# Half of the modulation weights on SyncE's queue, small transpositions ahead of the row products, and a split broadcast for batch 0

## The reference, cut to what matters

```python
mod = (_silu(L0_c) @ L0_wmod).reshape(B, 6, 1, -1)      # c: 4x256, wmod: 256x1536
sa, ca, ga, sb, cb, gb = (mod[:, 0], mod[:, 1], mod[:, 2], mod[:, 3], mod[:, 4], mod[:, 5])
ga = (2 * (ga >= 0) - 1) * jnp.maximum(jnp.abs(ga), 0.25)
gb = (2 * (gb >= 0) - 1) * jnp.maximum(jnp.abs(gb), 0.25)
h = _layernorm(x, axis=-1) * (1 + ca) + sa
x = x + ga * attn(h, Wq, Wk, Wv, Wo)      # mask: key column <= row + (132 - 1024)
h = _layernorm(x, axis=-1) * (1 + cb) + sb
x = x + gb * moe(h, ...)                  # shared expert + top 2 of 16 experts
```

## Time and profile before

| | |
|---|---|
| runs | 349.38 us median (348.1, 349.38, 352.21) |
| span of the profiled execution (its first to its last instruction) | 347.5 us |
| the executions' own times, around the span | 348.1 to 352.21 us; the page gives the span alone for the profiled one |
| busy share of the span | PE 80%, PEld 62%, DVE 67%, ACT 47%, POOL 59% |
| chain of waits, by engine | PE 54%, DVE 22%, DMA 7%, issue 7%, ACT 4%, POOL 2% |
| DMA | 59.80 MB, mean 172 GB/s |
| granted clock, mean | 0.913 |

### The profile page before, as it was taken

One profiled execution on the slowest core, in us unless ns is written; L12 is line 12 of the kernel. 1 busy time (PEld: TensorE's weight loads), 2 busy tenths in 40 slices (PEclk: granted clock), 3 DMA queues, 4 the chain that ended last, 5 costly groups with the idle time before them and its releaser, 6 DMA issues.

```text
span 347.5 us, 6287 instructions
## 1 busy us (share of the span) xinstructions
PE 278.8 (80%) x1665; PEld 215.0 (62%) x1666; DVE 231.3 (67%) x899; ACT 162.2 (47%) x518; POOL 205.2 (59%) x254
## 2 busy tenths in 40 slices
PE   4897889998988899989774999898899898886000
PEld 3264457656766576757543989787788787775000
DVE  0477477998889886997885645544345477763990
ACT  3142562278225822556222455454545566654550
POOL 3713116738784777558557356564655578875981
PEclk9996996999899996999988799999999999999555
DMA  7949001133624649702286644454456778869793
GB/s 261 330 132 347 16 2 49 59 100 115 197 80 135 183 127 320 163 30 93 72 228 205 201 138 121 144 177 133 138 160 180 245 210 254 263 188 343 247 360 139
DMA packets 41438, 59.80 MB, mean 172 GB/s; under 512 B 5092, under 2 KB 29880, under 8 KB 41404
## 3 DMA queue, kind: packets, MB, share of 16 engines
q1 hardware_dynamic: 34312, 39.91, 39.4%
q0 software_dynamic: 6528, 17.90, 14.3%
q10 hardware_dynamic: 564, 1.59, 1.4%
HBM read 33.57 MB, written 25.80 MB: 171 GB/s over the span
## 4 chain that ended last, share of the span: by engine, by line
PE 54%; DVE 22%; DMA 7%; issue 7%; ACT 4%; POOL 2%; another core or an unknown queue 1%; SPq 1%; DVEq 0%; POOLq 0%; ACTq 0%
PE bank L1227 16%; PE bank L892 8%; PE bank L1237 8%; PE bank L1085 6%; PE bank L1029 3%; PE bank L1052 3%; DVE bank L1752 3%; PE bank L1105 3%; DMA ht<-in_L_attn_x_dram 2%; PE bank L1067 2%; DVE h_sb L1369 2%; DMA ys<-pt_win,row_i 2%; PE bank L935 1%; PE bank L906 1%; DMA p_win<-slots 1%
## 5 line engine op out<-in xcount | busy, mean ns | idle before, releaser
L648 POOL DMA_INDIRECT ys<-pt_win,row_i x72 | 72.6, 1009 | 51.0 <-ACT pt_win L676 27.5
L1227 PE MATMUL bank<-ht,w_now 128*128 128x128 f32 x576 | 78.3, 280 | 4.4 <-issue 4.4
L593 POOL DMA_INDIRECT slots<-h_sb,slot_i x64 | 63.2, 987 | 30.1 <-issue 15.3
L1227 PEld LDWEIGHTS bank<-ht,w_now 128*128 128x128 f32 x576 | 71.7, 195 | 5.4 <-issue 5.1
L1741 DVE TENSOR_TENSOR act_t<-bank,sg 128x128 f32<-128x128 f32 x72 | 20.9, 290 | 48.5 <-ACT sg L843 33.2
L676 ACT ACTIVATE ht<-bank 128x256 f32<-128x256 f32 x104 | 39.9, 383 | 22.5 <-PE bank L892 15.6
L1237 PE MATMUL bank<-w_dn,act_t 128*128 x144 | 44.8, 393 | 5.4 <-DVE act_t L1741 4.3
L676 ACT ACTIVATE pt_win<-bank 128x256 f32<-128x256 f32 (+1 forms) x88 | 37.2, 423 | 21.7 <-PE bank L1237 9.6
L1085 PE MATMUL bank<-w_route,ht 128*128 128x272 f32 x128 | 41.5, 452 | 5.5 <-ACT ht L676 3.2
L892 PE MATMUL bank<-ident,p_win 128*128 128x128 f32 x198 | 36.1, 278 | 4.9 <-issue 3.2
L843 ACT ACTIVATE sg<-bank 128x128 f32<-128x128 f32 x72 | 20.1, 279 | 42.2 <-PE bank L1227 29.6
(11 more groups left out here) (260 smaller groups left out, 489.2 us busy)
## 6 DMA issues: line engine op xcount, KB each, us to landing
p_win<-slots SPq DMA_DIRECT2D x67, 129.0 KB
slots<-pads SPq DMA_DIRECT2D x28, 129.0 KB
xs<-in_L_attn_x_dram SPq DMA_DIRECT2D x3, 1024.0 KB
wmod_sb<-ys SPq DMA_DIRECT2D x12, 256.0 KB
w_gu<-ys SPq DMA_DIRECT2D x10, 256.0 KB, 2.8
mod_bc<-mod_rows_out SPq DMA_DIRECT2D x4, 512.0 KB, 5.7
w_dn<-in_L_ffn_w_down_dram SPq DMA_DIRECT2D x1, 2048.0 KB
h_sb<-ys SPq DMA_DIRECT2D x8, 256.0 KB
```

Source lines behind the costliest of these rows:

```text
L593: pool.indirect_dma_start(out=slots, out_offset=bass.IndirectOffsetOnAxis(ap=slot_i[:, k, j:j + 1], axis=0), in_=h_sb[:, j, :], in_offset= ...
L648: pool.indirect_dma_start(out=ys, out_offset=bass.IndirectOffsetOnAxis(ap=row_i[:, col:col + 1], axis=0), in_=y_sb[:, k, :], in_offset=Non ...
L1227: last = mm(bank[2 + k % 2][:, half * P:(half + 1) * P], w_now[:, k % 2, c, half * M:(half + 1) * M], ht[:, k, c, :], start=(c == 0), stop ...
```

## The change

1. The second half of w_mod (the row half, 1 MB) is loaded by SP, fifth in its order, behind the last tile and ahead of wq. ACT keeps the first half and `o_n`.
2. PE does at_tr(0) ahead of both row products, and no longer between them.
3. The broadcast of batch 0 is three DMAs: sb and cb together (256 KB, `mod_first`), then gb, then ga (128 KB each, new semaphore `mod_gates`). Batches 1 to 3 follow as before.
4. POOL waits for `mod_gates` before the `wsd_gated` of batch 0, and DVE before the `at_add` of batch 0.

```diff
         @block.sync
         def _(sp):
-            chunks = lambda w: w.rearrange("(c p) n -> p c n", p=P)
             sp.dma_start(cond_in[:], cond).then_inc(S["ld_cond"], 16)
...
             sp.dma_start(xcols(TPB - 1), x[0, T - P:T, :]).then_inc(S["ld_last"], 16)
+            sp.dma_start(wmod_sb[:, :, 2 * D:6 * D], chunks(w_mod)[:, :, 2 * D:6 * D]).then_inc(S["ld_wmod_rows"], 16)
             sp.dma_start(wq_sb[:], chunks(wq)).then_inc(S["ld_wqk"], 16)
...
             sp.wait_ge(S["mod_ready"], 1)
             sp.dma_start(mod_rows_out, mod[:, 2 * D:6 * D]).then_inc(S["mod_out"], 16)
             sp.wait_ge(S["mod_out"], 16)
-            for b in range(B):
-                sp.dma_start(mod_bc[:, b * 4 * D:(b + 1) * 4 * D], mod_rows_out[b:b + 1, :].to_broadcast([P, 4 * D]))\
-                    .then_inc(S["mod_in" if b > 0 else "mod_first"], 16)
+            sp.dma_start(mbc(0, SB_, 2), mod_rows_out[0:1, SB_ * D:(SB_ + 2) * D].to_broadcast([P, 2 * D]))\
+                .then_inc(S["mod_first"], 16)
+            for kind in (GB, GA):
+                sp.dma_start(mbc(0, kind), mod_rows_out[0:1, kind * D:(kind + 1) * D].to_broadcast([P, D]))\
+                    .then_inc(S["mod_gates"], 16)
+            for b in range(1, B):
+                sp.dma_start(mbc(b, 0, 4), mod_rows_out[b:b + 1, :].to_broadcast([P, 4 * D])).then_inc(S["mod_in"], 16)
...
                     pool.wait_ge(S["y_ps"], b * TPB)
+                if b == 0:
+                    pool.wait_ge(S["mod_gates"], 32)
                 pool.tensor_tensor(wsd_gated[:], wsd_sb[:], mbc(b, GB), ALU.mult).then_inc(S["wsd_ready"], 1)
...
         def _(act):
-            for cols, s in ((slice(0, 2 * D), "ld_wmod"), (slice(2 * D, 6 * D), "ld_wmod_rows")):
-                act.dma_start(wmod_sb[:, :, cols], w_mod[:, cols].rearrange("(c p) n -> p c n", p=P)).then_inc(S[s], 16)
+            act.dma_start(wmod_sb[:, :, 0:2 * D], chunks(w_mod)[:, :, 0:2 * D]).then_inc(S["ld_wmod"], 16)
             act.dma_start(sm_q, x[:, T - P - SINKS:T - P, :]).then_inc(S["ld_small"], 16)
...
+            at_tr(0)
             pe.wait_ge(S["ld_wmod_rows"], 16)
             for n in (1, 2):
                 for k in range(C):
                     last = mm(bank[4 + n][0:B, :], cond_t[:, k, :], wmod_sb[:, k, n * 2 * D:(n + 1) * 2 * D],
                               start=(k == 0), stop=(k == C - 1))
                 last.then_inc(S["setup_ps"], 1)
-                if n == 1:
-                    at_tr(0)
...
             def at_add(b, at):
                 dve.wait_ge(S["at_out"], b + 1)
+                if b == 0:
+                    dve.wait_ge(S["mod_gates"], 32)
                 at.done(v.tensor_tensor(o_g[:], bank[5][:, 0:D], mbc(b, GA), ALU.mult))
```

More of the change, by code:

```diff
@@ L292, in bass_adaln_attention_moe @@
         const setup_ps cond_ready mod_rows mod_ready ld_wmod_rows ld_last
-        col_ready mod_out mod_first mod_in sm_gate_sb
+        col_ready mod_out mod_first mod_gates mod_in sm_gate_sb
         sm_veps sm_rs sm_xnr sm_chain sm_hr sm_kqr sm_vr sm_ps sm_sub sm_exp sm_ptr
@@ L380, in table, with chunks @@
                 skip_runtime_bounds_check_because="the experts' numbers and tiles are clamped where the table is made")[1]
+        def chunks(w):
+            return w.rearrange("(c p) n -> p c n", p=P)
         block = ctx.enter_context(nc.Block())
```

## The result

| | before | after |
|---|---|---|
| median of 20 runs | 349.91 us | 347.46 us |
| lowest, highest | 347.06, 355.03 | 345.24, 351.86 |
| ratio after to before, 95% interval | | 0.9929 [0.9906, 0.9952] |
| span of the profiled execution | 347.5 us | 344.5 us |
| first h tile on DVE | 27.20 | 25.08 |

The kernel became faster by 2.5 us, 1.7 to 3.3 by the interval.

The account below looks back on a forecast made before the run. The setup's chain of waits, the first 28 us, was taken as the bound. Row products ending 1.4 us earlier, plus 0.1 for the column products, gave 1.5 off the 349.38 median: 347.9 us, range 344.6 to 350.6.

Parts of the forecast that it names:

- The small load: DVE's start in the setup: o_n lands at 5.7 us, DVE starts at 6.0 and not 8.57, both normalised inputs at 8.6.
- TensorE in order: TensorE ahead of the row products: column products from 5.3 to 8.9 us, then transpositions; row products start at 9.95, against 10.99.
- the row half: Second half of w_mod on SyncE's queue: issued at 3.49, landing at 9.3 us, hidden by 0.6; bounds 8.0 and 11.0.
- rival 3: L935's wait: row half, served together with loads behind it, lands at 13.9 us; time 351.9 us; chance 0.07.
- The row products, one slow and one fast: TensorE's eight records: 3.22 and 1.82 us again, ending at 14.99 against 16.41, 1.4 us earlier; bounds 13.6 and 16.4.
- The broadcast split, counted as nothing: First broadcast read, 256 KB less: 0.7 us shorter, but it only widens POOL's slack ahead of DVE's first h tile.
- The two new waits: POOL's wsd_gated at 40.20 and DVE's at_add at 60.16 wait for gates landing at about 25: no cost.
- the loads behind: SyncE's loads after the row half move back one place; cover 3 us at the least, nothing charged; queue drained by 17.5.
- Rival 1: Row products run fast throughout, as TensorE no longer idles ahead: end 13.6, gain 2.8, 346.6 us; chance 0.27.
- Rival 2: Order brings nothing, SyncE's small loads were late: row products end 16.7, 0.3 us later, 349.7 us; chance 0.08.
- Rival 4: Low-clock stretches from 27.3 us on shift: gain taken back, 349.4 us, chance 0.13; or 3 us added, 344.9, chance 0.05.

Follow-up runs that it names:

- after_again: The changed kernel, unaltered, measured again on a second chip: 345.52 us against 347.67 for the kernel before, ratio 0.9863.
- after_b: The changed kernel, unaltered, measured again on a third chip: 340.39 us against 342.49 for the kernel before, ratio 0.9988.
- rows_late: The changed kernel with the row half issued behind wq to gate_in and x of batch 0 on SyncE's queue: 357.61 us in its one run.
- split_only: The kernel before with only batch 0's broadcast split and the two waits for the gates: 347.08 us, ratio to before 1.0054.
- no_split: The changed kernel without the split of the broadcast and its two waits: 345.49 us, ratio to the kernel before 0.9974.
- order_only: The kernel before with only at_tr(0) put ahead of the row products: 348.51 us, ratio to before 1.0043.
- small_first: The kernel before with only o_n put between the two halves of w_mod on ScalarE's queue: 343.54 us, ratio to before 1.0009.
- load_only: The kernel before with only the row half of the weights moved to SyncE's queue: 348.04 us, ratio to before 0.996.
- load_only_2: The row half moved to SyncE's queue alone, a second time, on a third chip: 341.01 us, ratio to the kernel before 0.9979.
- warm: The changed kernel with seven unused TensorE transpositions ahead of the first real one: 347.14 us, ratio to the kernel before 0.9854.

## Why the prediction was right, and where not

The forecast was 347.9 us for 349.38, so 1.5 us; measured are 2.5 (1.7 to 3.3), and 347.46. That the two times agree within 0.5 us is in part luck: the gain was 1.0 larger than forecast, and the median of three runs that it was taken off was 0.5 below that of twenty. The range, 344.6 to 350.6, held the time of no change too, so it is the marks in the profile that bear the mechanism out. Its steps, against the profile of after and the two others of the same program (after_again, after_b):

| step | forecast | after | others |
|---|---|---|---|
| DVE's first operation | 6.0 | 6.23 | 5.75, 6.10 |
| column products start | 5.3 | 5.01 | 5.01, 5.01 |
| row half has landed | 9.3 | 9.45 | 9.46, 9.25 |
| row products start | 9.95 | 9.54 | 9.51, 9.48 |
| their end | 14.99 | 14.37 | 15.6, 15.2 |
| first broadcast, issue to landing | 3.5 | 3.0 | 3.0, 3.2 |
| first h tile | 25.7 | 25.08 | 26.30, 25.93 |

- *The small load, TensorE in order, the row half*: right, each within 0.4 us in after. The column products were the term that was too cautious: one issue fewer on ScalarE starts them 0.5 us earlier and not 0.2. The row half was hidden by 0.1 us rather than 0.6, and rival 3's price was the right one: one for one at the row products and the first h tile, shown by rows_late. Its mechanism is real too: loads issued behind the row half are served before it has landed. In after they cost little, with a landing of 6.1 us and 5.8 forecast.
- *The row products, one slow and one fast*: right in after and before. That it is a draw, and the same program takes 4.8 or 6.1 us, the bounds had and the point did not; that the profiled execution of after drew 4.83 is luck. With equally slow records (split_only and after_again, 6.11 and 6.08 us) the first h tile is at 28.21 and 26.30: 1.9 us is what the load and the order bring there beside the split, and the load alone brings 1.7 to 1.8.
- *The broadcast split, counted as nothing*: the mechanism of slack was right, DVE was last. But the sum missed that POOL's scaling lay under DVE's copy: 0.1 us in before's profile, 0.5 in no_split, order_only and small_first, nothing in load_only and load_only_2.
- *The two new waits, the loads behind*: nothing waited for them. One cover was thinner than I had it: the write of the rows was issued at 17.66, 0.5 us sooner than forecast, while the loads ended at about 18.2 and not 17.5; from its issue to the broadcast's it took 1.88 us, against 1.75 before. The slack of the broadcast hid that.
- *Rival 1* falls (warm, rows_late, after_again). *Rival 2* falls: DVE started earlier in every kernel with the new loads; its term, at_tr on the old loads, was 0.26 us against 0.3 forecast. *Rival 4*, the gain taken back or added to by a stretch of low granted clock, is not shown. The first such stretch moved along with the work, from 27.3 to 25.2:

```profile
25.20:32.40 7.20, 6.46 (x19) 4.23 (x20) 4.72 (x21) 2.13 (x6) 2.39 (x3) 0.54 1.00 347
```

Of 1.9 us at the first at_add 1.2 were left at the fourth in this pair, but no_split and order_only kept all of theirs. The setup's 1.9 to 2.1 us lie inside the measured interval; what makes the rest of the 2.5 is not shown.

## What to carry to other kernels

A semaphore that counts several loads is as late as the last of them, and here that was the small one behind 1.5 MB on its queue: put ahead of the last megabyte, it let DVE start 1.9 us earlier. Look at the other queue too: the megabyte there held up the last tile by about 2 us. Where two paths end together, read what comes in front of the last operation on both engines, and not only the wait by name: here half a microsecond lay in a copy that a POOL operation held up. Compare profiles at marks (first start of a step) between executions with the same pace of TensorE; with 5 to 10 us between executions, parts of 0.5 us are seen there and not in a median of 12. And take the parts alone before crediting the whole: at the marks, one moved load did all that three edits did.

## What the runs showed of the hardware that I had not expected

- Eight records of 512 columns took 4.83 to 6.14 us in executions of the same or nearly the same program, whatever TensorE had done before: 3.58 us of column records, those plus seven transpositions, or 6.79 us of nothing. The granted clock was shown as 1.00 through all of it; that part of them ran at the lower level (1.2 GHz) is read from their durations alone.
- DVE's copy of 64x64 elements took 0.20 us with POOL idle, and 0.72 to 0.76 us when a POOL scaling of 0.7 us had just begun at its start. Wherever a scaling was under way at its start, it ended 0.07 to 0.11 us after that scaling.
- A load of 1 MB on one queue delayed a 128 KB load on the other by about 2 us (6.0 and 5.6 us from issue to landing with it, 3.2 to 4.2 without), though only 36 KB stood ahead of the small one on its own queue.
- A load of 1 MB on SyncE's queue landed at 16.3 us, and one of 128 KB that was issued 0.6 us behind it on the same queue landed at 14.8. By 16.3 us 0.9 MB more had been moved than was issued up to the load of 1 MB.
